# Quantised 16-head cross-attention on one core: another order on VectorE in the second group, query scaling on ScalarE, the mask as two one-pass products

## The chip, the cores and the metric

The kernel runs on one core of a Trainium2 chip. It is one launch that computes four pairs of layers one after the other (eight stages). The metric is the device time of the launch in microseconds (us). The change touches the first stage alone, a cross-attention whose query and output projections are quantised to 8 bits.

## The reference, cut to what matters

x is 64 sequences of 64 tokens of 256 numbers, so 4096 rows; the context has the same shape. The first step of the network is x = x + attention(layernorm(x), context, mask):

```python
def _w8a8_linear(x, w, b):
    qx, sx = _dyn_quant(x)        # row maximum / 127, rounded to whole numbers
    qw, sw = _quant_weight(w)     # the same for each row of w
    y = jnp.einsum('bnc,oc->bno', qx, qw) * (sx * sw[:, 0])
    return y + b
q = _w8a8_linear(x, wq, bq).reshape(B, N, H, D).transpose(0, 2, 1, 3)   # 16 heads of 16
k = (cond @ wk.T + bk).reshape(B, L, H, D).transpose(0, 2, 1, 3)
v = (cond @ wv.T + bv).reshape(B, L, H, D).transpose(0, 2, 1, 3)
scores = jnp.einsum('bhnd,bhld->bhnl', q, k) * inv_sqrt_d + mask[:, None]
attn = jax.nn.softmax(scores, axis=-1)
o = jnp.einsum('bhnl,bhld->bhnd', attn, v)
return _w8a8_linear(o.transpose(0, 2, 1, 3).reshape(B, N, C), wo, bo)
```

## The kernel before, in words

The function is head_attention_stage (L2009); it is built twice, with quant=True for the first stage and quant=False for the seventh. The change alters the quantised form only. P is 128 partitions, S is 64 tokens, D is 256, C = 2 halves of D. The 4096 rows are cut into NU = 16 units of UNIT = 256 rows; a unit has GU = 2 groups of 128 rows (two sequences each). A group is numbered n = 2t + g for unit t and group g.

The steps of one group are: the scores product into two PSUM banks (scores_pe, L2307: first the mask, multiplied by the identity matrix, then the keys, spread out head by head, times the queries); the row maximum, negated (max_dve, L2337); the exponential, 16 instructions, one per head (exp_act, L2358); eight transposes (transpose_pe, L2365) and their copy to SBUF (transposed_act, L2373); the product with the values (apply_pe, L2382), which also gives the sums; the division, the value bias, and the quantisation of the result (result_dve, L2395); its transpose, copy, and output projection (result_pe L2432, result_act L2441, out_pe L2449); the scaling and addition to x (residual_dve, L2461).

The steps of the next units' inputs, once per unit, are: layer norm and quantisation of x (norm_dve, L2101), in the middle of which the reciprocal root is made by GpSimd (norm_pool, L2148, line L2150) and waited for at L2113; the transpose of the quantised rows (input_pe, input_act); the keys (keys_pe, keys_act L2169); the spreading of the keys over heads, half by ScalarE in two parts (spread_act, L2180) and half by VectorE (spread_dve, L2192); the query product (queries_pe, L2226), its scaling by sx and by swq and the addition of the bias bq (queries_dve, L2241: two instructions at L2248 and one at L2253), its transposes (transposed_queries_pe, L2282) and their copy with the factor 1/4 (q_copy, L2255); the values (values_pe, values_act L2270); and the addition of the output bias to x by GpSimd (bias_pool, L2455, line L2459), which waits for the quantised rows.

The order of the work is written out by hand, one function per engine (unit_pe L2517, unit_act L2549, unit_dve L2583, unit_gp L2606). Each is called for t = -2 to 17, and inside goes through g = 0 and g = 1; a step is left out where its unit does not exist. The units 2 to 13 run in a loop of two units per pass. Groups are pipelined: in step (t, g) the scores of group n are made, group n-1 goes through transposes, product with values and result, group n-2's result is transposed, and group n-3 is projected and added to x. All engines run their lists strictly in order; semaphores join them. VectorE's list for a unit is, in group 0: maximum of n, residual of n-3, queries of t+1, result of n-1, spread of t+1; in group 1: maximum of n, residual of n-3, result of n-1, norm of t+2. GpSimd's list is: bias of t+1, reciprocal root of t+2. ScalarE's list is, in group 0: copy of n-1's transposes, input copy, keys of t+1, exponential of n, result copy of n-2, first half of the spreading; in group 1: copy of n-1's transposes, query copy, second half of the spreading, exponential of n, result copy, values of t+1.

Two waits of TensorE matter below. apply_pe of group n waits until the residual of group n-2 has been read out of the same PSUM bank (L2386, semaphore y_used), and input_pe waits for the quantised rows (L2204). SyncE loads context and mask of a unit two units ahead (load_ctx, L2492). The program's names are those of the profile: att_pr are the exponentials, att_xn and att_qx the normalised and quantised rows, att_km the spread keys, att_qf the scaled queries.

## Time and profile before

| what | value |
|---|---|
| median of 3 runs | 4823.49 us (4823.29 to 4832.37) |
| the profiled execution, own time | 4825.63 us |
| its span | 4823.9 us |
| granted TensorE clock, mean over the span | 0.925 |
| TensorE matmul busy over the whole span | 4165.9 us (86%) |
| VectorE, ScalarE, GpSimd busy | 2612.3 (54%), 2046.6 (42%), 886.9 us (18%) |
| first stage: first VectorE instruction of the unit pipeline to the last | 34.68 us to 415 us after the start |

The rows of a profile name the engine (PE is TensorE's matmuls, PEld its weight loads, DVE VectorE, ACT ScalarE, POOL GpSimd), the line of the kernel, the output and the inputs. In a timeline a row begins with the start time and the time taken in us; xN says how many instructions are joined in it; a bracket tells how long the engine stood idle before it and what released it. The clock is 1.00 at the full 2.4 GHz and 0.50 at 1.2 GHz.

### The profile page before, as it was taken

Reading aid. Unit: us, or ns where it says so; the run is one execution under the profiler, and the core shown is the slowest. Engines: PE = TensorE matmul, PEld = TensorE weight load, DVE = VectorE, ACT = ScalarE, POOL = GpSimd, SP = SyncE. Lnnn points to the kernel's source line nnn. Section 1 sums busy time; section 2 is a strip of 40 time slices with the busy share of each in tenths; the row PEclk is TensorE's granted clock in tenths of the full one; section 3 lists DMA queues with packets and bytes.
Section 4 is the critical chain, followed back from the end, with each engine's and each line's share of the span. In section 5 each row is a group of like instructions: output and inputs, shape, how many; then the busy total and the mean of one; then the engine's idle time right before and its main releaser. Section 6 shows DMA issues by size and latency. Waiting matters only on the chain. (4 is left out here: it accounts for less than half of the span.)

```text
span 4823.9 us, 74274 instructions
## 1 busy us (share of the span) xinstructions
PE 4165.9 (86%) x25324; PEld 3358.8 (70%) x25324; DVE 2612.3 (54%) x5915; ACT 2046.6 (42%) x5270; POOL 886.9 (18%) x714
## 2 busy tenths in 40 slices
PE   5886999999896866999999998899989998887692
PEld 3554899999774754777778776677767776565671
DVE  5877989899474245444444443433333333776633
ACT  4775666666222423333333333333333332666140
POOL 1002333333001420000000000222212222000145
PEclk9987999999997976999999999899989999999596
DMA  2001000000001012000000000100010000000344
GB/s 61 14 16 42 1 0 0 0 0 1 29 20 38 0 51 88 5 6 5 6 6 6 6 1 10 60 10 9 5 52 10 9 9 20 12 13 7 99 135 130
DMA packets 100268, 119.29 MB, mean 25 GB/s; under 512 B 13776, under 2 KB 81200, under 8 KB 99760
## 3 DMA queue, kind: packets, MB, share of 16 engines
q1 hardware_dynamic: 93152, 97.25, 6.3%
q0 software_dynamic: 6864, 18.75, 1.5%
q8 instruction: 150, 2.46, 0.2%
q14 instruction: 102, 0.84, 0.1%
HBM read 93.03 MB, written 22.94 MB: 24 GB/s over the span
## 5 line engine op out<-in xcount | busy, mean ns | idle before, releaser
L1145 ACT ACTIVATE peer_tab<-peer_sims 128x128 f32<-128x128 f32 x1024 | 305.6, 393 | 0.0
L1152 POOL TENSOR_TENSOR peer_tab<-peer_sims 128x2048 f32<-128x2048 f32 x64 | 244.6, 3842 | 289.7 <-ACT peer_sims L1129 260.5
L1200 DVE SCALAR_TENSOR_TENSOR peer_tab<-peer_tab,peer_th 128x2048 f32<-128x2048 f32 x128 | 294.9, 2345 | 0.3
L1624 DVE COPY mha_ks<-bank 128x512 f32<-128x512 f32 x128 | 88.4, 690 | 352.3 <-PE bank L1589 349.8
L1217 PE MATMUL bank<-ident,peer_tab 128*128 128x128 f32 x2048 | 247.1, 274 | 20.0 <-DVE peer_tab L1200 20.0
L1217 PEld LDWEIGHTS bank<-ident,peer_tab 128*128 128x128 f32 x2048 | 233.8, 142 | 33.6 <-DVE peer_tab L1200 21.2
L1267 PE MATMUL bank<-peer_wd,peer_hh 128*128 128x256 f32 x1024 | 242.1, 380 | 1.8 <-DVE peer_hh L1258 1.8
L1729 PE MATMUL bank<-mha_wo,mha_oT 128*128 128x256 f32 x1024 | 242.1, 379 | 0.0
L1240 PE MATMUL bank<-peer_hT,peer_wg 128*128 128x256 f32 x1024 | 242.0, 379 | 0.0
L643 DVE TENSOR_TENSOR moe2a_b<-moe2a_a,bank 128x512 f32<-128x512 f32 x104 | 71.5, 687 | 296.9 <-PE bank L556 274.1
L631 POOL TENSOR_TENSOR moe2a_hh_lo<-moe2a_hh,moe2a_hh_hi 128x512 fp32r<-128x512 f32 x104 | 141.1, 1356 | 401.4 <-ACT moe2a_hh_hi L622 384.6
L643 DVE TENSOR_TENSOR moe2b_b<-moe2b_a,bank 128x512 f32<-128x512 f32 x96 | 66.0, 687 | 273.6 <-PE bank L556 252.4
L1240 PEld LDWEIGHTS bank<-peer_hT,peer_wg 128*128 128x128 f32 x1024 | 194.8, 190 | 26.5
L1267 PEld LDWEIGHTS bank<-peer_wd,peer_hh 128*128 128x128 f32 x1024 | 188.2, 190 | 24.9 <-DVE peer_hh L1258 2.6
L631 POOL TENSOR_TENSOR moe2b_hh_lo<-moe2b_hh,moe2b_hh_hi 128x512 fp32r<-128x512 f32 x96 | 130.8, 1362 | 373.5 <-ACT moe2b_hh_hi L622 364.7
L1729 PEld LDWEIGHTS bank<-mha_wo,mha_oT 128*128 128x128 f32 x1024 | 184.9, 190 | 19.8
L1617 ACT ACTIVATE mha_vs<-bank 128x512 f32<-128x512 f32 x128 | 76.4, 597 | 254.7 <-PE bank L1603 254.7
L1249 ACT ACTIVATE peer_a<-bank 128x512 f32<-128x512 f32 x128 | 76.0, 594 | 214.8 <-PE bank L1240 169.8
L622 ACT ACTIVATE moe2a_hh_hi<-moe2a_hh 128x512 fp32r<-128x512 f32 x104 | 65.7, 632 | 235.1 <-DVE moe2a_hh L648 215.0
L1612 ACT ACTIVATE mha_qs<-bank 128x512 f32<-128x512 f32 x128 | 76.6, 599 | 204.7 <-PE bank L1589 204.7
L1258 DVE TENSOR_TENSOR peer_hh<-peer_a,peer_cwT 128x512 f32<-128x512 f32 x128 | 122.0, 953 | 75.8 <-PE bank L1267 75.8
L2391 PE MATMUL bank<-att_vbd,att_pT 128*64 128x34 f32 x2048 | 81.3, 238 | 82.1 <-DVE x L2473 36.6
(518 smaller groups left out, 11081.4 us busy)
## 6 DMA issues: line engine op xcount, KB each, us to landing
m_y_rows<-moe_y SPq DMA_DIRECT2D x79, 128.0 KB, 1.7
att_ctxT<-in_ctxT_dram SPq DMA_DIRECT2D x32, 256.0 KB, 2.7
x<-in_x_dram SPq DMA_DIRECT2D x4, 1024.0 KB, 9.2
lin_ctxT<-in_ctxT_dram SPq DMA_DIRECT2D x16, 256.0 KB, 2.7
mem_ctxT<-in_ctxT_dram SPq DMA_DIRECT2D x16, 256.0 KB, 2.8
mem_ctx<-in_ctx_dram SPq DMA_DIRECT2D x16, 256.0 KB, 3.1
t_scratch<-mha_hTf SPq DMA_DIRECT2D x8, 512.0 KB, 4.7
moe2a_hTf<-t_scratch SPq DMA_DIRECT2D x8, 512.0 KB, 3.7
```

What stands on the lines that cost most here:

```text
L631: nc.gpsimd.tensor_tensor(out=hhs[1][:, j % 2, :], in0=hh[:, j % 2, :], in1=hhs[0][:, j % 2, :], op=ALU.subtract).then_inc(lo_ready, 1)
L643: nc.vector.tensor_tensor(out=b[:, j % 2, :], in0=a[:, j % 2, :], in1=U[j % 2][:], op=ALU.mult).then_inc(b_ready, 1)
L1145: i = nc.scalar.activation(tab[g][h][:, b * P:(b + 1) * P], sims[:, g, h, P:2 * P], ACT.Identity, bias=sims[:, g, h, b:b + 1])
L1152: nc.gpsimd.tensor_tensor(out=tab[g][h][:].rearrange("p (a b) -> p a b", b=P), in0=sims[:, g, h, P:2 * P].unsqueeze(1).broadcast_to([P, NB ...
L1200: nc.vector.scalar_tensor_tensor(out=tab[g][h][:], in0=tab[g][h][:], scalar=th[:, g, h:h + 1], in1=tab[g][h][:], op0=ALU.is_ge, op1=ALU.mu ...
L1217: i = nc.tensor.matmul(TB[n % 2][:, j * P:(j + 1) * P], tab[g][h][:, blk * P:(blk + 1) * P], core.ident[:], start=(j == 0 and h == 0), sto ...
L1240: i = nc.tensor.matmul(GB[p % 2][:, n * PU:(n + 1) * PU], wg[:, c, blk * P:(blk + 1) * P], hT[par][:, c, :], start=(c == 0), stop=(c == C ...
L1258: nc.vector.tensor_tensor(out=hh[:, p % 2, :], in0=a[:, p % 2, :], in1=cwT[:, par, 2 * p:2 * p + 2, :].rearrange("p b t -> p (b t)"), op=A ...
L1267: i = nc.tensor.matmul(YB[par][:, g * D:(g + 1) * D], hh[:, p % 2, n * PU + g * P:n * PU + (g + 1) * P], wd[:, 2 * p + n, :], start=(p == ...
L1624: nc.vector.tensor_copy(ks[:, s % 2, :], K[:]).then_inc(ks_ready, 1)
L1729: i = nc.tensor.matmul(Y[g // 2][:, (g % 2) * D:(g % 2 + 1) * D], oT[:, s % 2, g * P:(g + 1) * P], wo[:, s, :], start=(s == 0 and g % 2 == ...
L2391: i = nc.tensor.matmul(OB[g][64 * b:64 * b + 64, p * 2 * HV:(p + 1) * 2 * HV], pT[:, p, 64 * b:64 * b + 64], vbd[par][:, 2 * g + b, p, :, ...
```

## The change

1. Queries. queries_dve goes. queries_act takes its place on ScalarE, in group 0 after the keys and before the exponential: two copies of 128x256 with the factor sx, after which ScalarE waits for its own result (semaphore qf_ready) and frees the PSUM bank. The column scale and bias are applied later, in q_copy, where queries are transposed and a column is a partition: two instructions of 128x256 with a scale and a bias per partition in place of one of 128x512. Their columns swq_col and bq_col are made once before the units (columns_pe: four transposes; columns_act: three activations).
2. Mask. It is split into a high part (rounded to the one-pass fp32r type by ScalarE, mask_act) and a low part (the rest, by GpSimd, mask_pool), one unit ahead. scores_pe multiplies each with an fp32r identity: four fp32r products of 128x512 per group where two fp32 products stood. TensorE waits for the low part (lo_ready) in front of group 0's mask products.
3. Order. In group 1 VectorE does: residual of n-3, maximum of n, spread of t+1, norm of t+2, result of n-1. In group 0: maximum, residual, result. Norm also waits for qf_ready, since sx is now read by ScalarE.
4. mask_act stands on ScalarE in group 1 behind exponential and result copy, in front of the values; mask_pool stands first in GpSimd's list, in front of bias and reciprocal root.

The DMA transfers, their places and their waits stay as they are.

```diff
+        swq_col, bq_col = sb("swq_col", [P, C]), sb("bq_col", [P, C])
+        identr = sb("identr", [P, P], FP32R)
+        mask_hi = [sb(f"mask_hi{i}", [P, GU, S], FP32R) for i in range(2)]
+        mask_lo = [sb(f"mask_lo{i}", [P, GU, S], FP32R) for i in range(2)]
...
@@ norm_dve, in front of the row maximum sx
+            if some(t):
+                dve.wait_ge(qf_ready, t)
...
-    def queries_dve(dve, t):
-        q_chain.begin(t)
-        fwait_filled(dve, t, QUERIES)
+    def columns_pe(pe):
+        for c in range(C):
+            nc.tensor.transpose(OB[0][:, c * P:(c + 1) * P], swq[:, c * P:(c + 1) * P], core.ident[:])
+            i = nc.tensor.transpose(OB[1][:, c * P:(c + 1) * P], bq[:, c * P:(c + 1) * P], core.ident[:])
+        i.then_inc(cols_filled, 1)
...
+    def mask_act(act, t, par):
+        act.wait_ge(ctx_in[par], (t // 2 + 1) * n_ctx)
+        if some((t - 1) * GU):
+            act.wait_ge(scored, (t - 1) * GU)
+        nc.scalar.activation(mask_hi[par][:], mask[par][:], ACT.Copy).then_inc(hi_ready, 1)
+
+    def mask_pool(pool, t, par):
+        pool.wait_ge(hi_ready, t + 1)
+        if some((t - 1) * GU):
+            pool.wait_ge(scored, (t - 1) * GU)
+        nc.gpsimd.tensor_tensor(out=mask_lo[par][:], in0=mask[par][:], in1=mask_hi[par][:], op=ALU.subtract).then_inc(lo_ready, 1)
+
+    def queries_act(act, t):
+        fwait_filled(act, t, QUERIES)
         if some((t - 1) * 3 + LAST // 2 + 1):
-            dve.wait_ge(filled[LAST % 2], (t - 1) * 3 + LAST // 2 + 1)
-        F = FB[QUERIES % 2]
+            act.wait_ge(filled[LAST % 2], (t - 1) * 3 + LAST // 2 + 1)
         for g in range(GU):
-            i = nc.vector.scalar_tensor_tensor(out=qf[:, g, :], in0=F[:, g * D:(g + 1) * D], scalar=sx[:, g:g + 1], in1=swq[:],
-                                               op0=ALU.mult, op1=ALU.mult)
-        i.then_inc(q_chain.sem, 1)
-        dve.wait_ge(q_chain.sem, q_chain.next())
-        dve.sem_inc(emptied[QUERIES % 2], 1)
-        nc.vector.tensor_tensor(out=qf[:], in0=qf[:], in1=bq[:].unsqueeze(1).broadcast_to([P, GU, D]), op=ALU.add).then_inc(qf_ready, 1)
+            i = nc.scalar.activation(qf[:, g, :], FB[QUERIES % 2][:, g * D:(g + 1) * D], ACT.Copy, scale=sx[:, g:g + 1])
+        i.then_inc(qf_ready, 1)
+        act.wait_ge(qf_ready, t + 1)
+        act.sem_inc(emptied[QUERIES % 2], 1)
...
@@ q_copy
+        if quant:
+            for c in range(C):
+                i = nc.scalar.activation(qT[par][:, c, :], FB[k % 2][:, c * UNIT:(c + 1) * UNIT], ACT.Identity,
+                                         bias=bq_col[:, c:c + 1], scale=swq_col[:, c:c + 1])
+            i.then_inc(emptied[k % 2], 1)
+            return
...
@@ scores_pe
         if quant:
+            if g == 0:
+                pe.wait_ge(lo_ready, t + 1)
             for c in range(C):
-                nc.tensor.matmul(SB[g][c][:].rearrange("p (h k) -> p h k", k=S), core.ident[:],
-                                 mask[par][:, g, :].unsqueeze(1).broadcast_to([P, H8, S]), start=True, stop=False, skip_group_check=True)
+                for n, part in enumerate((mask_hi, mask_lo)):
+                    nc.tensor.matmul(SB[g][c][:].rearrange("p (h k) -> p h k", k=S), identr[:],
+                                     part[par][:, g, :].unsqueeze(1).broadcast_to([P, H8, S]), start=(n == 0), stop=False, skip_group_check=True)
...
@@ unit_act
                 keys_act(act, t + 1)
+                if quant:
+                    queries_act(act, t + 1)
...
+            if g == 1 and quant and exists(t + 1):
+                mask_act(act, t + 1, nxt)
             if g == 1 and exists(t + 1):
                 values_act(act, t + 1, nxt, 0)
...
@@ unit_dve
+            if g == 1 and quant and exists(t3):
+                residual_dve(dve, t3, p3, g3)
             if exists(t):
                 max_dve(dve, t, par, g)
-            if exists(t3):
+            if not (g == 1 and quant) and exists(t3):
                 residual_dve(dve, t3, p3, g3)
-            if g == 0 and quant and exists(t + 1):
-                queries_dve(dve, t + 1)
+            if g == 1 and quant and exists(t + 1):
+                spread_dve(dve, t + 1, nxt, KM_DVE)
...
+            if g == 1 and quant and exists(t + 2):
+                norm_dve(dve, t + 2)
             if exists(t1):
                 result_dve(dve, t1, p1, g1)
-            if g == 0 and quant and exists(t + 1):
-                spread_dve(dve, t + 1, nxt, KM_DVE)
...
-            if g == 1 and exists(t + 2):
+            if g == 1 and not quant and exists(t + 2):
                 norm_dve(dve, t + 2)
 
     def unit_gp(pool, t, par):
         if quant and exists(t + 1):
+            mask_pool(pool, t + 1, 1 - par)
             bias_pool(pool, t + 1)
```

## Rows read from the trace of the kernel before

**Rows 1.** Stretch, length, busy (count) of PE, PEld, DVE, ACT, POOL; clock, DMA.

```profile
57.60:400.30 342.70, 284.27 (x2104) 177.97 (x2101) 268.76 (x633) 249.82 (x886) 27.55 (x28) 0.92 0.05 14
```

**Rows 2.** Timeline, GpSimd: the reciprocal root, once per unit.

```profile
183.32 0.70 POOL L2150 TENSOR_TENSOR att_rstd<-att_ve,neghalf 128x2 f32<-128x2 f32 x1 [16.54 <-DVE att_ve L2112]
...
205.78 0.70 POOL L2150 TENSOR_TENSOR att_rstd<-att_ve,neghalf 128x2 f32<-128x2 f32 x1 [16.61 <-DVE att_ve L2112]
...
365.95 0.70 POOL L2150 TENSOR_TENSOR att_rstd<-att_ve,neghalf 128x2 f32<-128x2 f32 x1 [17.23 <-DVE att_ve L2112]
```

**Rows 3.** Waits from 50 to 400 us: who waited for whom, total us, times, longest.

```profile
PE bank L2391 <- DVE x L2473: 36.6, 12, 3.1
```

**Rows 4.** Timeline, one unit: start us, us taken, engine, line, operation [idle before].

```profile
206.52 0.88 DVE L2116 SCALAR_TENSOR_TENSOR att_xn<-x,att_mv,att_rstd 128x256 f32<-128x256 f32 x2 [0.81 <-POOL att_rstd L2150]
...
210.09 1.28 DVE L2343 TENSOR_REDUCE att_nmax<-bank 128x8 f32<-128x512 f32 x2
...
210.58 1.97 PE L2165 MATMUL bank<-att_ctxT,att_wkT 128*128 128x256 f32 x8
...
212.91 1.13 PE L2391 MATMUL bank<-att_vbd,att_pT 128*64 128x34 f32 x32
...
214.09 1.94 PE L2316 MATMUL bank<-att_mask,ident 128*128 128x512 f32 x4
...
215.95 1.94 PE L2324 MATMUL bank<-att_km,att_qT 128*64 128x512 f32 x8
...
217.56 2.28 DVE L2198 TENSOR_TENSOR att_km<-att_kT,att_hmask 128x2048 f32<-128x2048 f32 x1
...
219.13 1.08 ACT L2379 ACTIVATE att_pT<-bank 128x512 f32<-128x512 f32 x2 [0.58 <-PE bank L2369]
219.76 1.28 DVE L2343 TENSOR_REDUCE att_nmax<-bank 128x8 f32<-128x512 f32 x2
220.10 0.60 ACT L2260 ACTIVATE att_qT<-bank 128x512 f32<-128x512 f32 x1
220.57 1.70 ACT L2187 ACTIVATE att_km<-att_kT,att_hmask 128x256 f32<-128x256 f32 x4
...
221.16 0.47 DVE L2469 SCALAR_TENSOR_TENSOR att_y<-bank,att_so,att_swo 128x256 f32<-128x256 f32 x1
...
222.17 3.38 ACT L2362 ACTIVATE att_pr<-bank,att_nmax 128x64 f32<-128x64 f32 x16
...
222.56 1.60 PE L2391 MATMUL bank<-att_vbd,att_pT 128*64 128x34 f32 x32 [3.04 <-DVE x L2473]
...
224.20 0.26 DVE L2401 RECIPROCAL att_rsum<-bank 128x16 f32<-128x16 f32 x1 [1.99 <-PE bank L2391]
...
225.31 0.51 ACT L2447 ACTIVATE att_oT<-bank 128x256 bf16<-128x256 bf16 x1
...
227.12 0.74 DVE L2104 BATCH_NORM_STATS2 att_stats<-x 128x6 f32 x2
...
228.54 0.70 POOL L2150 TENSOR_TENSOR att_rstd<-att_ve,neghalf 128x2 f32<-128x2 f32 x1 [16.91 <-DVE att_ve L2112]
```

**Rows 5.** Timeline, a later stage: fp32r products of 128x512, two in a row.

```profile
3300.72 0.62 PE L556 MATMUL bank<-moe2a_hT_lo,moe2a_wg_hi 128*128 128x512 f32 x2
3301.18 0.62 PE L556 MATMUL bank<-moe2a_hT_hi,moe2a_wg_lo 128*128 128x512 f32 x2
```

**Rows 6.** Groups of ScalarE instructions by shape: busy us, mean ns.

```profile
L2176 ACT ACTIVATE att_kT<-bank,att_bk 128x256 f32<-128x256 f32 x32 | 13.4, 470 | 17.6 <-PE bank L2165 17.6
...
L815 ACT ACTIVATE moe2a_wu_hi<-moe2a_raw 128x128 fp32r<-128x128 f32 x2 | 0.5, 296 | 0.0
```

**Rows 7.** Groups of GpSimd instructions by shape: busy us, mean ns.

```profile
L2459 POOL TENSOR_TENSOR x<-x,att_bo 128x512 f32 x12 | 15.2, 1267 | 46.6 <-DVE att_qx L2133 46.6
...
L2158 POOL TENSOR_TENSOR att_rr<-att_r,att_rstd 128x2 f32<-128x2 f32 x16 | 3.1, 195 | 1.3
```

**Rows 8.** TensorE alone in one microsecond: busy, then granted clock.

```profile
223.00:224.00 1.00, 1.00 (x24) 0.50 0.00 0
```

More of the change, by code:

```diff
@@ L2065, in head_attention_stage @@
         qx, qf = sb("qx", [P, GU, D], BF16), sb("qf", [P, GU, D])
+        swq_col, bq_col = sb("swq_col", [P, C]), sb("bq_col", [P, C])
+        identr = sb("identr", [P, P], FP32R)
+        mask_hi = [sb(f"mask_hi{i}", [P, GU, S], FP32R) for i in range(2)]
+        mask_lo = [sb(f"mask_lo{i}", [P, GU, S], FP32R) for i in range(2)]
+        cols_filled, cols_ready, hi_ready, lo_ready = sem("cols_filled"), sem("cols_ready"), sem("hi_ready"), sem("lo_ready")
         so, rso, oq = sb("so", [P, 2 * GU]), sb("rso", [P, 1]), sb("oq", [P, D], BF16)
@@ L2069, in head_attention_stage @@
         norm_chain = Chain(sem("norm_chain"), 7)
-        q_chain = Chain(sem("q_chain"), 1)
         quantize_weights_block(core, name + "_qw", [(args["wq"], wqT, swq), (args["wo"], woT, swo)])
@@ L2239, in queries_pe, with columns_act @@
         i.then_inc(filled[QUERIES % 2], 1)
-    def queries_dve(dve, t):
-        q_chain.begin(t)
-        fwait_filled(dve, t, QUERIES)
+    def columns_pe(pe):
[3 more added lines that the diff above has]
+        i.then_inc(cols_filled, 1)
+    def columns_act(act):
+        act.wait_ge(cols_filled, 1)
+        nc.scalar.activation(identr[:], core.ident[:], ACT.Copy)
+        for col, src in ((swq_col, OB[0]), (bq_col, OB[1])):
+            i = nc.scalar.activation(col[:], src[:, 0:C * P].rearrange("p (c k) -> p c k", k=P)[:, :, 0], ACT.Copy, scale=float(HD) ** -0.5)
+        i.then_inc(cols_ready, 1)
@@ L2638, in _ @@
             pe.wait_ge(weights_in, n_in)
+            if quant:
+                columns_pe(pe)
             all_units(pe, unit_pe)
@@ L2643, in _ @@
             act.wait_ge(weights_in, n_in)
+            if quant:
+                columns_act(act)
+                act.wait_ge(cols_ready, 1)
             all_units(act, unit_act)
```

## The prediction, made before the change was run

> **What bounds the kernel now.** Only the first stage changes, so I read that stretch. Busy time by engine shows no engine full: over 342.7 us, some 15 units, TensorE is busy 284, VectorE 269, ScalarE 250 and GpSimd 28 us [rows 1]. A unit takes 22.83 us on the mean of eight (183.32 to 365.95) and 22.46 us in its quickest form (183.32 to 205.78) [rows 2]. The waits tell who holds whom: TensorE's product with the values stood 36.6 us, 12 times about 3 us, for VectorE's residual [rows 3]. The timeline of one unit says why: VectorE does one thing after another from 210.09 to 221.16 and only then the residual; TensorE idles 3.04 us in front of 222.56 [rows 4]. So VectorE's order closes the unit's loop: product, result, norm, maximum, residual, queries, result, spreading, maximum, residual, product. GpSimd sits in it with one reciprocal root, 0.70 us, for which VectorE waits 0.81 us [rows 4].
>
> **The change, part by part.**
>
> *Queries.* VectorE loses three instructions, about 1.6 us a unit (an estimate from 0.47 us for 256 columns [rows 4]). ScalarE gains two of 0.47 us [rows 6] in front of the exponential of group 0, and a wait for itself; behind it stand that exponential, the result copy and half the spreading. The maximum of group 0 comes later still (below), so this costs nothing while that is so; if not, 0.9 us. The transposed copy becomes two instructions of 0.47 us, issued in some 0.70 us where one took 0.47 (220.10 to 220.57) [rows 4, 6].
>
> *Mask product.* Four fp32 instructions occupy 214.09 to 215.95, 1.86 us [rows 4]. Two fp32r products of the same width take 0.46 us [rows 5], so four take 0.92: 0.94 us less in each group, all of it TensorE time. Bounds: 0.8 (no cost but the columns) and 1.24 (each pair at its full 0.62).
>
> *Order.* In group 1 the residual goes first, so the 3 us wait of TensorE goes. Spreading moves behind the maximum of group 1; TensorE needs it only in the next unit. Norm moves in front of the result.
>
> *The new wait, and what stands behind it.* GpSimd's list starts with the mask's low part, which waits for ScalarE's mask copy, which stands behind the exponential of group 1. Behind it in GpSimd's queue are the bias and the reciprocal root, and that root is what VectorE waits for in the middle of norm, now with the result and the next unit's maximum behind it. Before, the bias ran early and the root at once. TensorE too waits for the low part in front of the mask of group 0; behind it stand the scores, an output projection and the transposes of the last group.
>
> *The closed loop this makes*, in us, each term at the clock of its row. From the exponential of group 1: 3.14 (222.17 to 225.31); result copy 0.27 (its 0.51, less the 0.24 by which it starts before the 3.38 of the exponential are over) [rows 4]; mask copy 0.30 [rows 6] and 0.05 to pass it on; low part 0.50; bias 1.27 [rows 7]; root until VectorE goes on 0.74 (205.78 to 206.52) [rows 2, 4]; rest of norm 3.57 (206.52 to 210.09); result 2.92 (224.20 to 227.12); maximum 1.40 (219.76 to 221.16); residual until TensorE goes on 1.40 (to 222.56); product with the values and a result transpose 1.18 (212.91 to 214.09) [rows 4]; mask 0.92; scores, projection and transposes until ScalarE goes on 3.18 (215.95 to 219.13); their copy 0.97; query copy 0.70; half the spreading 1.60 (220.57 to 222.17) [rows 4]; then the next exponential. The sum is 24.11 us against 22.46: 1.65 us more per unit. The maximum of group 1 is ready nearly 2 us before ScalarE has finished this queue, so it does not set the time, and the result of the other group ends beside TensorE's scores.
>
> The low part, 128x128, is not in the trace: between 0.195 us (2 columns) and 1.27 (512 columns) [rows 7]; I take 0.50 on the line between, as 128 lies near the small end. The loop takes this one to one: -0.3 to +0.8 us a unit. The Trainium skill (GPSIMD Engine Reference, section 3.1) gives 4497 ns for 2048 columns of such an instruction, which is 0.28 us for 128; with that the loop would be 0.2 us shorter and the whole 3 us less. No row here has this width.
>
> *Sum.* Twelve unit periods run on this loop: 12 x 1.65 = 19.8 us. The start: norm of unit 1 already waits for the first mask copy, and unit 0 has the whole new wait with short groups behind it; walking the same terms through these units gives 5 us more than before (bounds 0 and 10). The end, units 14 and 15, has no norm any more but has the mask copy and the queries on ScalarE: 2 us (bounds -2 and +4). Columns are made while VectorE and the first norm run, on idle TensorE and ScalarE: nothing; 2 us without that cover. DMA transfers keep their places, and ScalarE asks for the mask a unit after its load is issued: nothing. Together +27 us. The profiled execution has 4825.63 us, its span 4823.9; changed it would be 4852.6. That execution lies 2.1 us over the median of 4823.49, so the median should be **4850.5 us**. The slow-clock stretches, 22.83 - 22.46 = 0.37 us a unit, are left as they are.
>
> *Clock.* After the 3.04 us gap the clock stands at 0.50 from 223 to 224 [rows 8]; the product at 222.56 takes 1.60 us where the one at 212.91 takes 1.13 [rows 4]. Laying the same terms along all four engines I find three gaps a unit: an estimated 3.5 us in front of group 0's mask, then 1.8 (transpose of the quantised rows) and 2.7 (product, for the residual). A stretch after the first falls on scores that have 5 us of slack, for VectorE is still in norm and result. One after the last falls on the loop. The Trainium skill (TensorE: Matmul & The Clock Gate, section "HAM oscillation — how this bites in real kernels") says that a TensorE fed in bursts with waits between drops to half clock and starts each burst slow. The trace agrees for the gap at 222.56; by that rule the sum would have another 24 us, the second rival below.
>
> **The rivals.**
>
> 1. *Faster: GpSimd does not hold the root.* If the low part is there before VectorE has the statistics, norm runs through. Point of decision, from the end of the maximum of group 1: exponential 3.14, copies 0.62 and low part 0.50, 4.26 together, against spreading 2.20 (217.56 to 219.76) and statistics 1.42 (227.12 to 228.54) [rows 4], 3.62 together. Then ScalarE and TensorE close the loop: exponential to low part 4.26; mask 1.0 with the hand-over; scores, projection and transposes 3.0; input transposes 0.3 (an estimate) and keys 2.0 (1.97 at 210.58) [rows 4]; keys and queries on ScalarE 1.65 (four of 0.47 less overlap) [rows 6]; exponential and result copy 3.4; hand-over, projection and transposes 1.7; copies and spreading 3.3: 20.6 us, 1.9 less than 22.46. Over 12 units -22: **4801 us**. For it: both idle waits of TensorE and 1.9 us of mask per unit go. Against it: the queue is strict, and the exponential cannot start before the maximum that stands in front of norm on VectorE: 4.26 is already over 3.62, and bias and root, 2.0 more, follow. Chance 0.13.
> 2. *Slower still: the half clock falls on the loop.* From product to transposes TensorE has 5.3 us on the loop; a third more of it (the one product at 222.56 took 42% more than the one at 212.91 [rows 4]) is 1.7 us a unit, over 14 units 24: **4874 us**. For it: the row on the clock, and by the layout above over 8 us of idle TensorE in 24. Against it: the gap in front of these 5.3 us is shorter than the 3.04 us behind which the clock was seen to fall, and most of the fall would come behind the first gap, where it costs nothing. Chance 0.13.
> 3. *No change that can be measured:* low part at 0.2 us (-4), the slow stretches gone with the 3 us gap (-5), start and end at nothing (-7), some overlap I don't see: +11 or a bit less, **4833 us**. Chance 0.09.
>
> **How the numbers follow.** The forecast, the 24.11 us loop with the clock as now, has 0.65; its own range is 4838 to 4864 (low part -4 to +11, start and end, errors of 0.3 us a loop). About 0.2%, 9.6 us, is what a measurement can tell from no change. Slower by more: 0.65 + 0.13 = 0.78. Within: 0.09. Faster by more: 0.13. The range goes from 4820, which takes in most of case 3, to 4875, which takes in case 2's value; left out are case 1 and the far ends of the others.
>
> **What would show it.** Right: the roots 24 us apart; VectorE idle 4 to 5 us in front of L2116's successor for the root, where it was 0.81; GpSimd's low part released by ScalarE's mask copy, with bias and root right behind it; TensorE idle some 3.5 us in front of the mask of group 0; the wait of L2391 for the residual still there, in group 0. Mask products at 0.23 us each. Wrong: roots under 22 us apart, or a wait for the root of 1 us. If the low part shows 1 us, the term was mis-sized, not the loop; if products on the loop stand at 0.50 in most units, it is case 2.

## The result, and the profile after

The changed kernel takes 4882.98 us (median of 4 runs, 4875.78 to 4895.19), the kernel before 4825.02 us beside it (4823.29 to 4832.37). The ratio is 1.012, interval 1.0094 to 1.0145: slower by 58 us, where 27 were forecast. The sign was right, the size half of what came; the median lies 8 us above the range. The profiled execution is the slowest of the four, 4895.19 us.

| what | value |
|---|---|
| profiled execution, its span | 4895.19 us, 4893.5 us |
| granted TensorE clock, mean | 0.919 |
| VectorE, ScalarE, GpSimd busy | 2589.8 (53%), 2069.3 (42%), 895.2 us (18%) |

First, where the time went. GpSimd's first instruction of the next stage marks the end of the changed one; the group rows by tile give it for the kernel before, then for the changed one (the two numbers after the durations are the first and the last start):

```profile
L1402 POOL MEMSET peer_bdk<- x1: 956/956/956, 417.7 to 417.7; 128x1024 f32 x1
```

```profile
L1402 POOL MEMSET peer_bdk<- x1: 957/957/957, 473.8 to 473.8; 128x1024 f32 x1
```

So 56.1 us of the span's 69.6 are in the changed stage; the other 13.5 arise in stages that both kernels have alike, and are about what this execution lies above its median.

The same stretch as in [rows 1], and the waits of that stretch, of the changed kernel:

```profile
57.60:400.30 342.70, 250.40 (x1828) 157.18 (x1825) 214.01 (x511) 235.06 (x823) 30.52 (x39) 0.85 0.05 13
```

```profile
POOL att_mask_lo L2270 <- ACT att_mask_hi L2264: 305.3, 13, 25.2
...
DVE att_xn L2120 <- POOL att_rstd L2156: 66.2, 13, 7.9
PE bank L2352 <- POOL att_mask_lo L2270: 47.6, 13, 3.9
```

All engines do less in the stretch because fewer units fit in. VectorE now waits for the root 66.2 us in 13 units, 5.1 us each where it was 0.81 [rows 4]; GpSimd waits for the mask copy, and TensorE 3.7 us a unit for the low part. These are the waits that the prediction named. But the clock is 0.85 where it was 0.92 [rows 1], and the prediction did not count on that.

Two units in a row of the changed kernel's timeline, a slow one and a quick one (VectorE, GpSimd and ScalarE only where the argument needs them):

```profile
202.91 0.46 POOL L2270 TENSOR_TENSOR att_mask_lo<-att_mask,att_mask_hi 128x128 fp32r<-128x128 f32 x1 [24.99 <-ACT att_mask_hi L2264]
...
214.90 1.93 PE L2427 MATMUL bank<-att_vbd,att_pT 128*64 128x34 f32 x32 [3.16 <-DVE x L2509]
...
216.92 0.78 PE L2352 MATMUL bank<-att_mask_hi,att_identr 128*128 128x512 f32 x1
...
218.90 2.79 PE L2360 MATMUL bank<-att_km,att_qT 128*64 128x512 f32 x8
...
230.44 0.46 POOL L2270 TENSOR_TENSOR att_mask_lo<-att_mask,att_mask_hi 128x128 fp32r<-128x128 f32 x1 [25.18 <-ACT att_mask_hi L2264]
230.85 1.28 POOL L2495 TENSOR_TENSOR x<-x,att_bo 128x512 f32 x1
231.03 0.76 PE L2352 MATMUL bank<-att_mask_hi,att_identr 128*128 128x512 f32 x1 [3.66 <-POOL att_mask_lo L2270]
...
232.08 0.70 POOL L2156 TENSOR_TENSOR att_rstd<-att_ve,neghalf 128x2 f32<-128x2 f32 x1
...
232.82 0.88 DVE L2120 SCALAR_TENSOR_TENSOR att_xn<-x,att_mv,att_rstd 128x256 f32<-128x256 f32 x2 [4.79 <-POOL att_rstd L2156]
...
239.31 1.28 DVE L2379 TENSOR_REDUCE att_nmax<-bank 128x8 f32<-128x512 f32 x2
...
241.86 1.13 PE L2427 MATMUL bank<-att_vbd,att_pT 128*64 128x34 f32 x32 [2.57 <-issue]
...
243.02 0.48 PE L2352 MATMUL bank<-att_mask_hi,att_identr 128*128 128x512 f32 x1
...
244.12 1.94 PE L2360 MATMUL bank<-att_km,att_qT 128*64 128x512 f32 x8
...
248.26 1.02 ACT L2289 ACTIVATE att_qT<-bank,att_bq_col,att_swq_col 128x256 f32<-128x256 f32 x2
...
254.86 0.46 POOL L2270 TENSOR_TENSOR att_mask_lo<-att_mask,att_mask_hi 128x128 fp32r<-128x128 f32 x1 [22.08 <-ACT att_mask_hi L2264]
```

From one low part to the next, the quick unit takes 254.86 - 230.44 = 24.42 us; the forecast loop was 24.11. The slow one takes 230.44 - 202.91 = 27.53. Of the difference of 3.1 us most lies on TensorE: behind its wait for the residual the product takes 1.93 us against 1.13, the four mask products 1.98 (216.92 to 218.90) against 1.10 (243.02 to 244.12), the scores 2.79 against 1.94. That is 2.5 us; the other 0.6 lies on VectorE, from the end of norm until the residual lets TensorE go on (6.05 us against 5.45). The windows view of four and of three us in these two units (the number behind POOL's is the clock):

```profile
217.00:221.00 4.00, 4.00 (x12) 1.73 (x12) 2.62 (x8) 1.97 (x5) 0.00 (x0) 0.54 0.00 0
243.00:246.00 3.00, 3.00 (x15) 1.17 (x16) 2.73 (x8) 3.00 (x11) 0.00 (x0) 1.00 0.00 0
```

At 0.54 the engine is nearly all the time at 1.2 GHz, at 1.00 it is at 2.4. From the fifth root of this trace on, two units take 24.4 us and nine 26.5 to 27.5. TensorE's wait before the product of group 0 is 1.82 to 3.16 us long; in four of the nine slow units it is only 1.82 to 1.87 us, the product runs at full clock and the slow stretch begins in the mask products behind it. So the theory after the result: the loop costs about what was forecast, and the half clock behind the wait for the residual falls on that loop and costs the other half. Rival A: something else on the loop is longer and the clock only goes along. Rival B: the wait for the low part, not the one for the residual, brings the costly half clock.

### The profile page after: what moved, and what is told of

Its sections match the earlier page's. It is cut to its first block and busy times, and to the rows that moved or that the text cites. A ratio compares the mean times of both kernels' runs of the same rounds, so it can differ in the third digit from the quotient of the medians.

```text
span 4893.5 us, 74376 instructions
## 1 busy us (share of the span) xinstructions
PE 4175.5 (85%) x25328; PEld 3367.6 (69%) x25328; DVE 2589.8 (53%) x5867; ACT 2069.3 (42%) x5337; POOL 895.2 (18%) x730
## 5 line engine op out<-in xcount | busy, mean ns | idle before, releaser
L1217 PE MATMUL bank<-ident,peer_tab 128*128 128x128 f32 x2048 | 247.9, 275 | 24.4 <-DVE peer_tab L1200 24.4
```

Of the source, the lines that this page charges most:

```text
L1217: i = nc.tensor.matmul(TB[n % 2][:, j * P:(j + 1) * P], tab[g][h][:, blk * P:(blk + 1) * P], core.ident[:], start=(j == 0 and h == 0), sto ...
```

## The experiments

Each kernel differs from the changed one ("after") or from the one before by what its diff shows. "Unit" is the mean distance of 13 roots of GpSimd (third to last), "stage end" the start of L1402. The difference and the ratio are against the kernel before, run on the same chip beside it (its medians there: 4835.35 us for e1 to e4, 4833.24 for e5 to e8, 4827.47 for e9 to e12). Where an expectation speaks of the first, second, third or seventh run, it means e1, e2, e3 or e7.

| kernel | unit, us | clock 120-330 | stage end | median | to before | ratio |
|---|---|---|---|---|---|---|
| before | 22.78 | 0.92 | 417.7 | | | |
| after | 26.24 | 0.82 | 473.8 | 4882.98 | +58.0 | 1.012 |
| e1 GpSimd's mask step last | 23.87 | 0.87 | 434.6 | 4855.93 | +20.6 | 1.0035 |
| e2 mask copy early | 22.17 | 0.91 | 407.1 | 4826.86 | -8.5 | 0.9981 |
| e3 filler at both waits | 24.63 | 1.00 | 448.5 | 4868.98 | +33.6 | 1.0071 |
| e4 mask product of before | 23.48 | 0.93 | 422.2 | 4843.90 | +8.6 | 1.002 |
| e5 e1 with filler | 21.78 | 1.00 | 403.2 | 4825.66 | -7.6 | 0.9984 |
| e6 order alone | 23.23 | 0.94 | 422.0 | 4838.27 | +5.0 | 1.0013 |
| e7 e2 with residual early | 20.86 | 0.96 | 389.5 | 4804.43 | -28.8 | 0.9943 |
| e8 order of before | 22.95 | 0.93 | 423.6 | 4843.14 | +9.9 | 1.002 |
| e9 residual early alone | 24.19 | 0.91 | 448.6 | 4861.87 | +34.4 | 1.0069 |
| e10 e4 with residual early | 20.75 | 1.00 | 387.7 | 4799.60 | -27.9 | 0.9942 |
| e11 e6 with residual early | 21.04 | 1.00 | 391.9 | 4805.94 | -21.5 | 0.9955 |
| e12 filler before the product | 24.67 | 0.92 | 450.7 | 4863.50 | +36.0 | 1.0073 |

The stage's end moves with the median in every kernel, within 7 us, so what follows is told by unit and clock.

### The loop through GpSimd: e1, e2, e8

**e1.** The mask step behind the root in GpSimd's list:

```
         if quant and exists(t + 1):
-            mask_pool(pool, t + 1, 1 - par)
             bias_pool(pool, t + 1)
         if exists(t + 2):
             norm_pool(pool, t + 2)
+        if quant and exists(t + 1):
+            mask_pool(pool, t + 1, 1 - par)
```

> As the changed kernel, but GpSimd does bias, reciprocal root and then the mask's low part. Nothing is left out. Theory (the closed loop through GpSimd's queue): the root no longer stands behind ScalarE's exponential, the loop opens, VectorE's wait for the root falls from 4.8 us to about 0.8, and ScalarE with TensorE close a loop of 20.7 us at full clock; the first stage gets some 20 us shorter than before the change: 4800 to 4815 us. Rival A (ScalarE's longer list and TensorE's wait for the low part set the time, not the root): the units stay at 24 us or more, 4850 to 4885 us. Rival B (the slow clock is what costs, and it follows TensorE's wait for the low part, which stays): units of 23 us or more, 4825 to 4850 us.

Measured: 4855.93 us, ratio 1.0035 (1.0021 to 1.0049), 23.87 us a unit. Moving one 0.46 us instruction takes 37 us off the changed kernel, so the place in the queue is a cause. VectorE's idle time before the normalised rows is 0.81 us again, as in [rows 4]. But the theory's 20.7 us a unit did not come. The timeline says why:

```profile
283.20 0.80 PE L2352 MATMUL bank<-att_mask_hi,att_identr 128*128 128x512 f32 x1 [3.54 <-POOL att_mask_lo L2270]
...
285.20 3.68 PE L2360 MATMUL bank<-att_km,att_qT 128*64 128x512 f32 x8
```

Mask products and scores together take 5.7 us (283.20 to 288.88), 2.6 us more than at full clock (1.10 + 1.94 above), in every unit. The time, 4855.93 us, is in the stretch of the rival that named another loop, but the trace speaks for the clock; e5 below tells them apart.

**e2.** ScalarE's mask copy out of group 1 into group 0:

```
                 if KM_ACT:
                     spread_act(act, t + 1, nxt, 0)
+                if quant:
+                    mask_act(act, t + 1, nxt)
...
-            if g == 1 and quant and exists(t + 1):
-                mask_act(act, t + 1, nxt)
```

> As the changed kernel, but ScalarE copies the mask's high part in group 0, behind the first half of the spreading, half a unit earlier. GpSimd's order is as in the changed kernel. Nothing is left out. Theory: both waits, VectorE's for the root and TensorE's for the low part, go, with the place in GpSimd's list unchanged; 20.4 us a unit at full clock, 4790 to 4810 us. Rival A (ScalarE's length): units at 24 us, 4850 to 4885. If this and the kernel with the late low part come out alike, TensorE's wait for the low part cost nothing by itself.

Measured: 4826.86 us, ratio 0.9981 (0.9972 to 0.9991), 22.17 us a unit, root wait 0.81 us. The low part runs at 258.00 us for a mask that is used at 264.28 us. One instruction moved takes the changed kernel from +58 to -8.5 us: the copy's place behind the exponential of group 1 closed the loop. The expectation's size again was missed, and again with TensorE at half clock, here behind 2.57 us of idling:

```profile
253.29 1.92 PE L2427 MATMUL bank<-att_vbd,att_pT 128*64 128x34 f32 x32 [2.57 <-issue]
```

**e8.** The changed kernel with VectorE's order of before; ScalarE's query scaling, the mask in two parts and GpSimd's list stay:

```
-            if g == 1 and quant and exists(t3):
-                residual_dve(dve, t3, p3, g3)
             if exists(t):
                 max_dve(dve, t, par, g)
-            if not (g == 1 and quant) and exists(t3):
+            if exists(t3):
                 residual_dve(dve, t3, p3, g3)
-            if g == 1 and quant and exists(t + 1):
-                spread_dve(dve, t + 1, nxt, KM_DVE)
...
-            if g == 1 and quant and exists(t + 2):
-                norm_dve(dve, t + 2)
             if exists(t1):
                 result_dve(dve, t1, p1, g1)
+            if g == 0 and quant and exists(t + 1):
+                spread_dve(dve, t + 1, nxt, KM_DVE)
...
-            if g == 1 and not quant and exists(t + 2):
+            if g == 1 and exists(t + 2):
                 norm_dve(dve, t + 2)
```

> The changed kernel with VectorE's order of before (maximum, residual in both groups; spreading in group 0; result, then norm, at the end); query scaling on ScalarE, the mask in two parts and GpSimd's order (low part, bias, root) stay as changed. Theory (the loop closes only with the new order, since only there does the norm stand in front of the result): 22.4 to 22.9 us a unit, clock about 0.92 as in the kernel before, ratio to the kernel before 0.998 to 1.001. Rival (mask copy and low part cost on their own, wherever the norm stands): 23.5 us a unit or more, ratio 1.003 or more.

Measured: 22.95 us a unit, ratio 1.002 (1.0011 to 1.003). The unit is as expected to 0.05 us (22.78 before); the ratio is 0.001 over, and of the 5.9 us at the stage's end 5.1 arise before the third root (74.90 against 69.81 us), where the first mask copy is waited for. In the old order the late copy, the low part and the queries on ScalarE cost 0.2 us a unit all together; e8 does not show what each does by itself. So the loop of 24.4 us a unit needs the new order as well as the places of low part (e1) and copy (e2).

### The clock on the loop: e3, e12, e9

**e3.** TensorE is given work in both waits, 7 products of 128x128 by 128x256 before the mask of group 0 and 4 before the product of group 0 (their results are overwritten by what follows, nothing is left out):

```
+            if g == 0 and quant and exists(t2):
+                pe.wait_ge(on_ready, t2 * GU + g2 + 1)
+                fill_pe(pe, OB[g2][:, 0:D], 4)
             if exists(t1):
                 apply_pe(pe, t1, p1, g1)
...
                 values_pe(pe, t + 1, nxt, 1)
+                if quant:
+                    fill_pe(pe, SB[0][0][:, 0:D], 7)
```

> As the changed kernel, with additional fp32 products of 128x256, whose results nobody reads, where TensorE waits: seven in front of the mask of group 0 (some 3.1 us of its 3.6 us gap) and four in front of the product with the values in group 0 (1.8 us of 2.6), behind a wait for the quantised result that is there by then. Theory (loop of 24.1 to 24.4 us, the rest is the half clock that follows the gaps): with TensorE kept busy the clock stays at 1.00, all units take 24.4 us as two of fourteen do now, against a mean of 26.6: about 28 us less than the changed kernel, 4850 to 4860 us. Rival (the difference between units of 24.4 and 27 us has another cause and the clock only goes with it): units stay at 26 to 27 us on the mean, 4875 to 4895 us.

Measured: 4868.98 us, ratio 1.0071 (1.0055 to 1.0088), clock 1.00. Units are 24.4 and 24.9 us in turn. With 11 products more for TensorE in each unit the kernel is 24 us quicker. The time is between the two expected stretches; the unit decides, and with the clock full it has the forecast's length, so rival A is out.

**e12.** Only the four products before the product of group 0.

```
+            if g == 0 and quant and exists(t2):
+                pe.wait_ge(on_ready, t2 * GU + g2 + 1)
+                fill_pe(pe, OB[g2][:, 0:D], 4)
             if exists(t1):
                 apply_pe(pe, t1, p1, g1)
```

> The changed kernel with four more products on TensorE right before the group-0 product alone (behind its wait for the result of the unit before), none before the mask. The third run had these and seven before the mask: clock 1.00 and 24.7 us a unit. Theory (the wait in front of the group-0 product, for the residual, is what turns the clock down before mask and scores of the next group, and the wait in front of the group-0 mask does the same for group 0, so each costs some 1 us a unit): 25.2 to 26 us a unit, clock 0.88 to 0.95, ratio to the kernel before 1.008 to 1.010. Rival (only the wait before the mask matters): 26 to 26.6 us a unit, ratio above 1.010. Rival (only the wait before the product matters): 24.4 to 25 us a unit, ratio 1.006 to 1.008.

Measured: 4863.50 us, ratio 1.0073 (1.0056 to 1.0089), 24.67 us a unit, clock 0.92. My own theory fell here, and the last rival stands: only the wait before the product matters. The timeline shows both places:

```profile
246.14 0.80 PE L2352 MATMUL bank<-att_mask_hi,att_identr 128*128 128x512 f32 x1 [3.62 <-POOL att_mask_lo L2270]
...
248.14 2.60 PE L2360 MATMUL bank<-att_km,att_qT 128*64 128x512 f32 x8
...
254.62 1.99 PE L2367 MATMUL bank<-att_wkT,ident 128*128 128x256 f32 x8 [0.15 <-DVE att_oq L2469]
...
257.62 1.13 PE L2431 MATMUL bank<-att_vbd,att_pT 128*64 128x34 f32 x32 [1.00 <-DVE x L2513]
...
259.87 1.94 PE L2360 MATMUL bank<-att_km,att_qT 128*64 128x512 f32 x8
```

The scores of group 0 (248.14) still run slow behind 3.62 us of idling, and this costs no time, as the prediction said of them. Those of group 1 (259.87) are on the loop and run at full clock. Where half clock falls decides, not how much of it there is: e12 has 0.92 and e3 1.00, at the same unit. So the wait for the low part alone does not bring the costly half clock (rival B), and e2 above shows it with the wait for the residual alone. Whether the wait for the low part has a share in the four slow units with a short wait for the residual stays open: e5 below, where it is filled, keeps full clock behind waits of up to 1.85 us before the product. No run fills the wait before the mask alone in the changed kernel.

**e9.** No filler: VectorE's residual of group n-3, for which the product of group 0 (that of group n-1) waits, is moved from behind the maximum of group 0 to between norm and result of the unit before. The mask copy stays late.

```
-            if not (g == 1 and quant) and exists(t3):
+            if not quant and exists(t3):
                 residual_dve(dve, t3, p3, g3)
...
                 norm_dve(dve, t + 2)
+            if g == 1 and quant and exists(t - 1):
+                residual_dve(dve, t - 1, nxt, 1)
             if exists(t1):
                 result_dve(dve, t1, p1, g1)
```

> The changed kernel with one move alone: VectorE's residual of group 0 between the norm and the result at the end of the unit before (ScalarE's mask copy stays late, so the loop through the low part is closed). Theory (the loop is what holds the unit, and the slow clock on it comes from the waits of TensorE in front of product and mask; this takes away the first and leaves the second, for the low part): 24 to 24.5 us a unit at full clock, 24.5 to 25.5 as it runs, root wait over 4 us in each unit, ratio to the kernel before 1.004 to 1.008. Rival (the residual was the whole trouble, the loop is none without it): 20.5 to 21.5 us a unit, ratio below 0.997. Rival (moving it does nothing while the loop is closed): as the changed kernel, 26.5 us a unit, ratio 1.010 or more.

Measured: 4861.87 us, ratio 1.0069 (1.0052 to 1.0085), 24.19 us a unit. The product of group 0 now starts without a wait and takes 1.13 us; VectorE still waits for the root:

```profile
244.26 0.50 PE L2352 MATMUL bank<-att_mask_hi,att_identr 128*128 128x512 f32 x1 [3.62 <-POOL att_mask_lo L2270]
...
246.14 0.88 DVE L2120 SCALAR_TENSOR_TENSOR att_xn<-x,att_mv,att_rstd 128x256 f32<-128x256 f32 x2 [4.98 <-POOL att_rstd L2156]
...
252.53 1.13 PE L2427 MATMUL bank<-att_vbd,att_pT 128*64 128x34 f32 x32
...
259.00 0.39 PE L2488 MATMUL bank<-att_woT,att_oT 128*128 128x256 bf16 x2 [2.15 <-ACT att_oT L2483]
```

The loop takes another course here: the product is done before VectorE's maximum, and the loop goes on through ScalarE's exponential of group 0 and the result copy behind it, for which TensorE waits at 259.00 us. So e9 shows how long the unit is without the wait for the residual, but not the forecast's loop term by term; e3 and e12 keep that loop.

Two ways to the same place, by work put into the wait (e12) and by the wait taken away (e9), leave +33.0 and +30.9 us at the stage's end of the changed kernel's +56.1. e3 leaves +30.8. What is gone, 23 to 25 us, is the clock's part; what is left is the loop.

### The clock in the open loop: e5, e4, e6

**e5** is e1 with filler before the mask of group 0:

```
                 values_pe(pe, t + 1, nxt, 1)
+                if quant:
+                    fill_pe(pe, SB[0][0][:, 0:D], 6)
```

> The changed kernel with GpSimd's order bias, root, low part (as in the first run), and six more 128x128 products on TensorE right before the group-0 mask products, so that TensorE works while it would wait for the low part. Theory (the first run's 23.87 us a unit was the slow clock on mask and scores, nothing else): granted clock 0.95 to 1.00, 20.7 to 21.5 us a unit, the peer stage begins 15 to 30 us before that of the kernel before, ratio to the kernel before 0.993 to 0.997. Rival (another loop holds 23.9 us, and the clock only goes along with it): clock 1.00 and still 23.5 to 24 us a unit, ratio 1.002 to 1.004. Rival (the added products stand on the loop themselves, 6 x 0.27 us): 22 to 22.5 us a unit, ratio 0.998 to 1.000.

Measured: 4825.66 us, ratio 0.9984 (0.9974 to 0.9993), clock 1.00, units of 21.3 and 21.9 us. Against e1 this is 28 us less, with six more products a unit: e1's 23.87 us was the half clock. The rival that the loop is longer by itself is out. The unit is 0.3 us over the theory's upper end and the ratio over its 0.997. The third case does not explain this: the six products take 2.7 us and not 6 x 0.27, but TensorE still waits 0.9 to 1.1 us for the low part behind them, so they are not on the path. The first of the 13 distances, 23.81 us, makes some 0.2 us of it.

**e4** is the changed kernel with the fp32 mask product of before, without mask copy and low part:

```
-            if g == 0:
-                pe.wait_ge(lo_ready, t + 1)
             for c in range(C):
-                for n, part in enumerate((mask_hi, mask_lo)):
-                    nc.tensor.matmul(SB[g][c][:].rearrange("p (h k) -> p h k", k=S), identr[:],
-                                     part[par][:, g, :].unsqueeze(1).broadcast_to([P, H8, S]), start=(n == 0), stop=False, skip_group_check=True)
+                nc.tensor.matmul(SB[g][c][:].rearrange("p (h k) -> p h k", k=S), core.ident[:],
+                                 mask[par][:, g, :].unsqueeze(1).broadcast_to([P, H8, S]), start=True, stop=False, skip_group_check=True)
...
-            if g == 1 and quant and exists(t + 1):
-                mask_act(act, t + 1, nxt)
...
-            mask_pool(pool, t + 1, 1 - par)
```

> As the changed kernel, but the mask product is the one of before, two fp32 products and no split, so neither ScalarE nor GpSimd nor TensorE has anything to do for the mask. New order and queries on ScalarE stay. Theory: without the low part in front of bias and root the loop is open; 21.3 us a unit at full clock, 4800 to 4820 us. Rival A (the new order or ScalarE's queries are what costs): units of 24 us or more, over 4850 us.

**e6** is the kernel before with VectorE's new order and nothing else:

```
+            if g == 1 and quant and exists(t3):
+                residual_dve(dve, t3, p3, g3)
             if exists(t):
                 max_dve(dve, t, par, g)
-            if exists(t3):
+            if not (g == 1 and quant) and exists(t3):
                 residual_dve(dve, t3, p3, g3)
             if g == 0 and quant and exists(t + 1):
                 queries_dve(dve, t + 1)
+            if g == 1 and quant and exists(t + 1):
+                spread_dve(dve, t + 1, nxt, KM_DVE)
+            if g == 1 and quant and exists(t + 2):
+                norm_dve(dve, t + 2)
...
             if exists(t1):
                 result_dve(dve, t1, p1, g1)
-            if g == 0 and quant and exists(t + 1):
-                spread_dve(dve, t + 1, nxt, KM_DVE)
...
-            if g == 1 and exists(t + 2):
+            if g == 1 and not quant and exists(t + 2):
                 norm_dve(dve, t + 2)
```

> The kernel before with nothing changed but VectorE's order in group 1 (residual, maximum, half spreading, norm, result); query scaling stays on VectorE, the mask is the one fp32 product of before, GpSimd has no mask step. Theory (the loop through GpSimd's low part is what costs 24.4 us a unit, the order alone closes none; but the order puts the 3 us wait of TensorE for the residual in front of the group-0 product, and the slow clock behind it): 21.3 us a unit where the clock is full, 23 to 24 us as it runs, ratio to the kernel before 0.999 to 1.003. Rival (the order alone is the gain and the clock does not care): 21.3 us a unit throughout, ratio 0.995 to 0.998. Rival (the order alone is the loss): over 24 us a unit, ratio 1.006 to 1.012.

Measured: e4 4843.90 us, ratio 1.002 (1.001 to 1.003), 23.48 us a unit; e6 4838.27 us, ratio 1.0013 (1.0004 to 1.0022), units of 23.4 and 24.0 us in turn, and twice 21.8. e4 missed its expectation, made before the clock was understood; e6, made after, met it. The two are alike, and neither has a mask step on GpSimd, so what both still lack is not the loop's. e6's timeline:

```profile
262.37 1.13 PE L2391 MATMUL bank<-att_vbd,att_pT 128*64 128x34 f32 x32 [3.19 <-issue]
...
263.55 3.49 PE L2316 MATMUL bank<-att_mask,ident 128*128 128x512 f32 x4
```

The fp32 mask product of group 1 takes 3.49 us where it took 1.94 in [rows 4]. In the kernel before the same 3 us of idling stood in front of the other group's product, and the next mask product came 4.6 us later at full speed (222.56 and 227.12 us in its trace). The new order moves it to a place where mask, scores, maximum and exponential follow. In the two units of 21.8 us the product, the mask and the scores of group 1 all run at full clock; 21.8 against 22.8 before is what the order brings, and the half clock undoes it.

### Both removed: e7, e10, e11

**e7** has the edits of e2 and e9 together.

> The changed kernel with ScalarE's mask copy moved forward into group 0, behind its first half spreading (second run), and VectorE's residual of group 0 moved from behind the maximum of group 0 to between the norm and the result at the end of the unit before, so that TensorE's product of group 0 does not wait for it. Theory (the 3 us gap of TensorE in front of the group-0 product is that residual, and the half clock follows it): no gap over 2 us there, granted clock 0.95 or more, 19.9 to 20.8 us a unit, the peer stage begins 25 to 37 us before that of the kernel before, ratio 0.992 to 0.995. Rival (the gap moves to another wait, the clock stays at 0.92): 21.5 to 22.5 us a unit, ratio 0.997 to 0.999. Rival (result and maximum come later by the residual and hold the exponentials): over 22.8 us a unit, ratio above 1.000.

Measured: 4804.43 us, ratio 0.9943 (0.9929 to 0.9956): 28.8 us less than the kernel before, 87 less than the changed one by their differences. The theory held: 20.6 and 20.7 us a unit in the steady stretch, no wait over 1.3 us before the product of group 0 and none over 2.2 us elsewhere on TensorE. Ten units of it:

```profile
120.00:330.00 210.00, 164.68 (x1406) 111.72 (x1402) 175.78 (x407) 179.26 (x635) 23.80 (x30) 0.96 0.06 16
```

VectorE and ScalarE are 84% and 85% busy.

**e10** is e4 with the residual early, **e11** is e6 with it; the edit is that of e9 (in e11 the early residual stands in front of the result in the same way).

> The changed kernel with the mask again as one fp32 product per half (no mask copy, no low part) and the residual of group 0 early as in the seventh run. It tells what the mask's two one-pass products are worth once nothing else holds the unit. Theory (the unit is then held by VectorE and ScalarE, 85% busy, and not by TensorE): 20.5 to 21 us a unit like the seventh run, clock 0.95 or more, ratio to the kernel before 0.993 to 0.996. Rival (the 1.8 us of the fp32 mask stand on the path of scores, maximum, exponentials): 21.5 to 22.3 us a unit, ratio 0.996 to 0.999.

> The kernel before with VectorE's new order and the residual of group 0 early; query scaling stays on VectorE, the mask is the fp32 product, GpSimd has no mask step. It tells whether the order is all that is needed. Theory (VectorE was 0.80 busy at 22.8 us a unit, so with its query scaling it has 18.3 us of work and can hold 21 us): 20.8 to 21.6 us a unit, ratio to the kernel before 0.994 to 0.997. Rival (VectorE's query scaling behind the maximum lies on the path query, transposes, scores): 22 to 22.8 us a unit, ratio 0.998 to 1.000.

Measured: e10 4799.60 us, ratio 0.9942 (0.9925 to 0.9958), 20.75 us a unit, clock 1.00. The same as e7 within the intervals, so the two one-pass mask products bring nothing once the order is right: TensorE has time for the 1.9 us. e11 4805.94 us, ratio 0.9955 (0.9938 to 0.9972), 21.04 us a unit: the query scaling on ScalarE, which e10 has and e11 has not, is worth 0.3 us a unit, and the intervals of the two ratios overlap. Of the 28 us gained, 21.5 come from VectorE's order alone, with the residual early. Whether the early residual would do as much in VectorE's order of before was not tried.

## Why the prediction was right in sign and half in size

**The wait and the loop: right.** Five of the six signs named for it are there: low part released by the mask copy with bias and root right behind, VectorE idle 4.8 us for the root, TensorE idle 3.7 us before the mask of group 0, the residual's wait in group 0, the mask products 0.23 us apart at full clock (243.33, 243.56, 243.80). The sixth, roots 24 us apart, is there in two of eleven units only; the sign named for case 2, products on the loop at 0.50 in most units, is there in the other nine. The quick unit of 24.42 us checks the terms:

- low part and bias to the root, 1.64 us (230.44 to 232.08) against 1.77; the low part itself 0.46 against the 0.50 taken. The 0.28 us worked out for this width from the figure of the Trainium skill (GPSIMD Engine Reference, section 3.1) is too low here;
- root, rest of norm and result, 0.74 and 6.49 us (232.08, 232.82, 239.31), exactly as summed;
- maximum 1.40, residual until TensorE goes on 1.15 (239.31, 240.71, 241.86), against 1.40 and 1.40;
- mask 1.10 against 0.92;
- the query copy 0.90 (248.26 to 249.16) against 0.70;
- the mask copy and its hand-over to the low part 0.69 (254.17 to 254.86) against 0.35. Longer and shorter terms together leave 0.3 us.

**The sum without the clock: nearly right.** e3, with the clock full and the forecast's loop, gives it: 13 x (24.63 - 22.78) = 24.1 us in the steady part (forecast 19.8 for twelve units), 5.1 us at the start (its third root at 74.86 us against 69.81; forecast 5) and 1.7 us at the end (L1402 starts 53.4 us behind the last root against 51.7; forecast 2). Together +31 against +27. e9 comes to the same +31 by its other course: 18.3, 6.6 and 6.0 us. One reading in the sum was off by a little: 22.46 us is not the quickest unit of the kernel before, whose trace has one of 22.27.

**The step that failed** is the clock's: "The slow-clock stretches, 22.83 - 22.46 = 0.37 us a unit, are left as they are." They were not. The mean unit of the changed kernel is 26.24 us, 1.8 over its own quick unit and 1.6 over those of e3 and e12 (24.63 and 24.67), and at the stage's end e3, e9 and e12 are 23 to 25 us ahead of it. The second rival had place, mechanism and price: "the half clock falls on the loop", 1.7 us a unit, 24 us, 4874 us. It was given 0.13, for two reasons in the text. The first, that "the gap in front of these 5.3 us is shorter than the 3.04 us behind which the clock was seen to fall", rested on a gap laid out by hand, 2.7 us, which came as 1.82 to 3.16 us, with half clock behind the short ones too. A difference of 0.3 us in an estimate cannot carry odds of five to one, and one row does not show how short a gap is harmless. The second, that "most of the fall would come behind the first gap, where it costs nothing", was half right: it does fall there and costs nothing (e12), but the clock falls at both places in one unit. Rival 2's price was right on the mean, 24 us against 23 to 25; a slow unit costs 2.1 to 3.1 us and not 1.7, but not every unit is slow. The Trainium skill (TensorE: Matmul & The Clock Gate, section "HAM oscillation — how this bites in real kernels") says that a TensorE fed in bursts starts each burst slow; its case is one of longer waits, for DMA. The trace agrees in part: nine of eleven units have a slow stretch behind the wait (in five of them the product itself takes 1.93 us against 1.13), two have none. The sum by that rule, +51 us, was nearer than the forecast.

**Rival 1** needed the low part ahead of the statistics; it starts 2.4 us behind them (230.44 against 228.03), and with bias and root VectorE waits 4.8 us. Its 20.6 us for the loop without GpSimd, though, is near the 20.6 to 20.9 us that e7 and e10 reach, once the residual too is out of the way. Its terms were not followed there, so that may be chance. **Rival 3** needed a low part of 0.2 us and the slow stretches gone; neither came.

The range ended at 4875, the value of case 2 itself, with nothing above it. Case 2 with start and end as the changed kernel has them (5.2 and 6.0 us, 11 and not 7) would be 4878. A range that takes in a case must take in its spread.

## What to carry to other kernels

When an order is changed, follow the idle time of TensorE as well as the critical chain: ask for each wait that remains which instructions come right behind it, and cost those at half clock if somebody waits for them. A short step that waits for a late one, put at the head of an in-order queue, makes everybody behind it in that queue late too; moving the 0.46 us step, or the copy it waits for, was worth 37 to 66 us here. And try an order with the one instruction moved that keeps TensorE waiting before the rest is judged: e6 and e11 differ by that alone, and by 27 us.

## What the runs showed of the hardware that was not expected

- More work made the kernel faster. e3 and e5 add 11 and 6 products a unit, and are 24 and 28 us quicker than the kernels without them.
- The same idle time did not always have the same effect. Behind 2.57 us before the product the clock was full in the changed kernel at 241.86 us (1.13 us) and half at 187.00 us (1.93 us), and half in e2 (253.29 us, 1.92 us). In e6 everything ran at full clock behind 3.20 us (309.86 us); in the changed kernel the mask products were slow behind 1.86 us (from 268.61 us on, 0.63 us each and not 0.39), and in e5 nothing was behind 1.74 us (274.56 us). What else goes into it was not settled by these runs.
- Whether the slow speed shows already in the first product behind the wait varies too: in e6 the product at 262.37 us runs at full speed behind 3.19 us of idling, and the mask product behind it takes 3.49 us. So the operation that follows a wait must be looked at together with the next two or three.
